# Two groups of PV products in a row every eight units, and three buffers of probabilities, in an attention and mixture-of-experts kernel

## What is computed

```python
def _L0_xattn_ref(x, c, Wq, bq, Wk, bk, Wv, bv, Wo, bo):
    q = einsum('oc,bct->bot', Wq, x) + bq        # k and v likewise, from c
    scores = einsum('bhkt,bhks->bhts', q, k) * SCALE
    p = softmax(scores, axis=-1)
    out = einsum('bhts,bhks->bhkt', p, v)
    return einsum('oc,bct->bot', Wo, out) + bo
x = x + _L0_xattn_ref(_layernorm(x), ctx, ...)   # B=8, C=256, T=512, 16 heads, 16 channels each
x = x + _L0_ffn_ref(_layernorm(x), ...)          # rmsnorm, top 2 of 8 experts, a shared expert
```

## Time and profile before

| | |
|---|---|
| median of three executions | 947.64 us (944.26 to 954.04) |
| the profiled execution's own time | 947.91 us |
| its span | 946.1 us |
| TensorE (PE) matmuls | 876.4 us, 93% of the span |
| VectorE (DVE) | 474.9 us, 50% |
| ScalarE (ACT) | 411.1 us, 43% |
| GpSimd (POOL) | 223.5 us, 24% |
| mean granted TensorE clock | 0.945 of full speed |

### The profile page before, as it was taken

How to read it: one execution, slowest core, us unless ns; L and a number is a source line. 1 busy time by engine, 2 the same in 40 slices (tenths; PEclk the granted TensorE clock), 3 DMA queues, 4 the chain that set the end, 5 groups by cost and what they waited for, 6 DMA issues and landing times. The chain is left out here.

```text
span 946.1 us, 10745 instructions
## 1 busy us (share of the span) xinstructions
PE 876.4 (93%) x3575; PEld 378.9 (40%) x3575; DVE 474.9 (50%) x915; ACT 411.1 (43%) x769; POOL 223.5 (24%) x206
## 2 busy tenths in 40 slices
PE   7798988999999999999998989987999999999992
PEld 2333423434333343333432245833544444444441
DVE  4496687687776777777784056183221111111110
ACT  1113566767667676666667741210002222222220
POOL 3113023104142031421100121000004444444431
PEclk8897899999999999999997987698999999999997
DMA  6777265456555565645611139300633555555542
GB/s 232 185 186 184 46 144 144 94 109 159 121 130 126 116 161 126 125 121 112 138 39 38 36 90 368 155 1 0 224 132 68 91 92 92 93 93 90 94 81 34
DMA packets 46872, 110.43 MB, mean 117 GB/s; under 512 B 11668, under 2 KB 12692, under 8 KB 42580
## 3 DMA queue, kind: packets, MB, share of 16 engines
q1 hardware_dynamic: 35404, 80.23, 33.6%
q0 software_dynamic: 11328, 29.37, 15.3%
q10 hardware_dynamic: 88, 0.16, 0.1%
HBM read 68.44 MB, written 41.16 MB: 116 GB/s over the span
## 5 line engine op out<-in xcount | busy, mean ns | idle before, releaser
L749 DVE TENSOR_REDUCE negmax<-smax_ps 128x1 f32<-128x512 f32 x512 | 323.4, 681 | 120.6 <-PE smax_ps L623 120.4
L549 ACT ACTIVATE probs<-st_ps 128x512 f32<-128x512 f32 x512 | 279.3, 600 | 172.5 <-PE st_ps L656 172.0
L656 PE MATMUL st_ps<-q_stack,k_stack 50*128 50x512 f32 x512 | 160.1, 501 | 13.2 <-ACT probs L549 10.9
L623 PE MATMUL smax_ps<-k_stack,q_stack 48*128 48x512 f32 x512 | 145.7, 445 | 15.1 <-DVE negmax L749 8.8
L669 PE MATMUL pv_ps<-probs,v_t 128*32 128x512 f32 x1024 | 141.2, 624 | 0.6 <-ACT probs L549 0.4
L1178 PE MATMUL big_ps<-w_gu,attn 128*128 x312 | 140.4, 593 | 0.8 <-ACT attn L1019 0.8
L656 PEld LDWEIGHTS st_ps<-q_stack,k_stack 50*128 50x128 f32 x512 | 61.5, 188 | 189.4 <-ACT probs L549 149.0
L983 POOL DMA_INDIRECT out<-x_sb,row_i x39 | 61.7, 1582 | 139.5 <-ACT x_sb L1026 132.4
L623 PEld LDWEIGHTS smax_ps<-k_stack,q_stack 48*128 48x128 f32 x512 | 68.0, 190 | 48.8 <-DVE negmax L749 33.6
L1364 DVE TENSOR_TENSOR zeros<-attn,big_ps 128x256 f32<-128x256 f32 x39 | 16.4, 421 | 134.8 <-ACT attn L1038 134.8
L1178 PEld LDWEIGHTS big_ps<-w_gu,attn 128*128 128x128 f32 x312 | 56.2, 190 | 57.0 <-issue 57.0
(11 more groups left out here) (156 smaller groups left out, 760.9 us busy)
## 6 DMA issues: line engine op xcount, KB each, us to landing
parts_dram<-parts SPq DMA_DIRECT2D x32, 512.0 KB, 6.2
k_stack<-parts_dram SPq DMA_DIRECT2D x32, 256.0 KB, 4.7
q_stack<-parts_dram SPq DMA_DIRECT2D x32, 256.0 KB, 5.3
w_gu<-in_gate_up SPq DMA_DIRECT2D x8, 1024.0 KB, 15.0
x_sb<-in_x SPq DMA_DIRECT2D x8, 512.0 KB, 7.8
c_sb<-in_ctx POOLq DMA_DIRECT2D x8, 512.0 KB, 7.8
k_stack<-parts_dram SPq DMA_DIRECT2D x32, 128.0 KB, 5.1
q_stack<-parts_dram SPq DMA_DIRECT2D x32, 128.0 KB, 5.9
```

What stands on the lines that cost most here:

```text
L549: nc.scalar.activation(probs[:, k % 2, u % GH, :], score_bank(UNITS * s + u), ACT.Exp, scale=SCALE).then_inc(exp_done, 1)
L623: nc.tensor.matmul(smax_bank(i), q_stack[buf][low:low + SROWS, pair, tt * P:(tt + 1) * P], k_stack[buf][low:low + SROWS, pair, :], start=T ...
L656: nc.tensor.matmul(score_bank(i), k_stack[buf][low:end, pair, st * P:(st + 1) * P], q_stack[buf][low:end, pair, :], start=True, stop=True, ...
L749: nc.vector.tensor_reduce(negmax[:, n % 2, c:c + 1], smax_bank(UNITS * n + u), AX_X, ALU.max, negate=True).then_inc(max_done, 1)
```

## The change

`probs` gets three buffers of one group each instead of two, and the exponentials of group k wait for `pv(k - 3)`. TensorE no longer does one group at every fourth unit, but two groups one right behind the other at every eighth: at u = 2, 10, 18 and 26, behind the two scores and the maxima of that step and ahead of whatever else hangs on it. The two copies of `pv_ps` move three units later, from after units 2 and 18 to after units 5 and 21. At the end the last two groups are done behind the loop instead of the last one.

```diff
@@ -27,6 +27,7 @@
 STBUF = 3
+PBUF = 3
@@ -108,7 +109,7 @@
-        probs = asb("probs", [P, 2, 4, T])
+        probs = asb("probs", [P, PBUF, GH, T])
@@ -544,13 +545,13 @@
                         k = STEPS * s + u // GH
-                        if u % GH == 0 and k >= 2:
-                            act.wait_ge(pv_done, k - 1)
-                        nc.scalar.activation(probs[:, k % 2, u % GH, :], score_bank(UNITS * s + u),
+                        if u % GH == 0 and k >= PBUF:
+                            act.wait_ge(pv_done, k - PBUF + 1)
+                        nc.scalar.activation(probs[:, k % PBUF, u % GH, :], score_bank(UNITS * s + u),
                                              ACT.Exp, scale=SCALE).then_inc(exp_done, 1)
-                        if u == 2 and s > 0:
+                        if u == 5 and s > 0:
                             pv_copy(2 * s - 1)
-                        if u == 18:
+                        if u == 21:
                             pv_copy(2 * s)
@@ -667,7 +668,7 @@
-                                              probs[:, k % 2, j, :], start=(st == 0), stop=(st == TT - 1),
+                                              probs[:, k % PBUF, j, :], start=(st == 0), stop=(st == TT - 1),
@@ -706,7 +707,8 @@
-                        if u % GH == 0 and STEPS * s + u // GH >= 1:
+                        if u % (2 * GH) == 2 and STEPS * s + u // GH >= 2:
+                            pv(STEPS * s + u // GH - 2)
                             pv(STEPS * s + u // GH - 1)
@@ -721,6 +723,7 @@
                             filler(smax_bank(0))
+                pv(STEPS * HALVES - 2)
                 pv(STEPS * HALVES - 1)
```

## The result

The changed kernel takes 1087.93 us, the median of four executions (1086.85 to 1091.95), against 947.71 before: a ratio of 1.148 (95% interval 1.141 to 1.155). It is 140 us slower. The forecast was 1109 us, 161 slower, from two terms: waits (67) and a falling clock (94).

The account below looks back on a forecast made before the run. PE, busy 93%, looked like the bound, but its narrow stretches were held to ACT's and DVE's pace. 947.9 us plus 67 of waits plus 94 of falling clock gave 1109 us (chance 0.71), range 1000 to 1150.

Parts of the forecast that it names:

- waits: PE held to ACT's and DVE's pace in long narrow stretches: 4.9 us a half over 12 halves, +67 us in all.
- a falling clock: PE's clock falls behind three long narrow stretches a half, slowing the next wide block by 2.6 us: +94 us (61 to 126).
- Rival 1: The clock holds in the attention loop and only the waits cost: 1015 us, 997 with small waits; chance 0.18.
- Rival 2: PE is the bound and the loop gets faster by 1.9 us a half, 27 us in all: 921 us; chance 0.03.
- switches: Changes on PE between narrow products and PV blocks: some 0.3 us saved for each block removed, 1.3 per half.
- Rival 3: The clock does not come back within a block, all wide work slow, 15 us more a half: 1195 us; chance 0.06.
- The account by rows: Sum of PE's blocks and narrow stretches in a half: 32.2 us after the change against 28.8 before, extras not included.
- The extras: ACT's and DVE's work beside units, now uncovered in long stretches (residual, statistics, copies): 1.5 us a half (0 to 2.7).
- my lower bound of 61: The low end, in us, of the range 61 to 126 given for the falling clock's cost.
- Halves 0 and 1: The first two halves of the loop, left at no added waits because DVE paces them already.
- The copies' later place: Copies of pv_ps come some 4 us later; DVE may wait for the denominators: nothing, at most 1 us a half.
- The tail: Last half and the extra PV group behind the loop 6 us, half 14 another 2: 8 us, counted in the waits.

Follow-up runs that it names:

- experiment 2: The changed kernel plus three full-width products of zeros a half, at u = 14, 24 and 30 in the long stretches: 1037.62 us, ratio 1.093 to the kernel before.
- experiments 5 and 6: 5: maxima and exponentials over half or a quarter of the columns, both kernels, 55 and 23 us apart; 6: kernel before with projections split and spread, 930.64 us.
- cut4_after: The changed kernel with VectorE's maxima and ScalarE's exponentials over a quarter of the columns: 916.47 us, against 893.63 for the kernel before with the same cut.
- cut_after: The changed kernel with VectorE's maxima and ScalarE's exponentials over half of the columns: 961.46 us, against 906.43 for the kernel before with the same cut.

## Why the prediction was right

**Direction and mechanism** held: waits and a falling clock, both through the order of wide and narrow work on PE. Rival 1 (the clock holds, 1015 us) fell with the granted clock of 0.85 and with experiment 2. Rival 2 (PE is the bound and gets its switches back, 921) fell with the result, and experiments 5 and 6 agree. Rival 3 (the clock stays low through whole blocks, 3.5 us or more in each) did not happen: no block with a projection is more than 2.84 us too long.

**The stretches.** The account by rows gave 4.39 us for eight units and 1.95 for four. The short ones around the projection at u = 6 read 1.94 in the changed kernel (360.37 to 362.31, and 364.22 to 366.16), as forecast. The block of a pair and a projection is 3.77, as forecast, and the pair in it 1.85 up to the projection (372.84 to 374.69), against the 1.86 that rested on an estimate of the last matmul's latency. The long ones of eight units between two such blocks are 4.45 to 5.25 us in even halves and 5.58 to 5.89 in odd ones. The extras, which I had put at 1.5 us a half, are 0.8 to 1.5 in even halves and 3 in odd ones (sum of the three long stretches less 3 x 4.39 and the turn), where the residual and its statistics lie in the stretch:

```profile
389.56 0.74 DVE L330 SCALAR_TENSOR_TENSOR x_sb<-proj_ps,bo_all,x_sb 128x512 f32<-128x512 f32 x1
...
391.42 0.68 DVE L794 BATCH_NORM_STATS2 stats<-x_sb 128x6 f32<-128x512 f32 x1
```

**The clock** was the term that I sized too high. I took 2.6 us for each of 36 long stretches, from blocks at half speed as in half 0: behind its narrow stretch of 4.5 us the granted clock is 0.50, also over the group at 88.11 alone (88.10 to 90.00), while the kernel before has 1.00 from 150 to 500 us, with narrow stretches like that of 1.94 in the earlier trace rows. From the turn of half 2 (175.72) to that of half 14 (643.38), 12 halves, PE's timeline has 34 blocks of a pair and a projection (from half 13 on no more keys are projected, so two of the 36 carry none). Five take 3.77 or 3.78 us. The other 29 are longer, 21 by 1.2 to 1.7 us and eight by 2.6 to 2.8. In the eight the slow level reaches into the projection, which takes 1.98 at a granted clock of 1.00; in the one below the clock is 0.50 over the pair and 0.68 over the projection (397.04 to 399.90):

```profile
393.47 3.64 PE L670 MATMUL pv_ps<-probs,v_t 128*32 128x512 f32 x16
397.04 2.89 PE L596 MATMUL proj_ps<-c_sb,w_t 128*128 128x512 f32 x4
```

Together they are 53 us too long, 1.5 for each of the 34. Four of the 14 pairs that stand alone add 6. That is 59 us against the 94 forecast, just under my lower bound of 61. No long wait of PE goes with these falls: from 176 to 500 us, at a mean granted clock of 0.86, its longest single wait is 0.71 us.

**The waits** were sized right. The 12 halves take 467.66 us against 351.68 (161.72 to 513.40), 116 more. Without the 59 that leaves 57, or 4.8 us a half, against the 59 and 4.9 forecast. It holds also what the slow clock costs inside the narrow stretches, which is not separated here. Experiment 2 agrees: its 12 halves take 421.59, and 8 us of that are blocks and fillers at the slow level, so without the slow clock they are 62 over the kernel before, fillers included. That the forecast comes so close is in part luck: at full clock a half of the changed kernel takes 34.1 us where I had 33.7, and the kernel before 29.3 where my account had 28.8, and the two errors cancel.

**What I left at nothing.** Halves 0 and 1: the turn of half 2 comes at 175.72 us instead of 161.72, 14 us late. The granted clock from 64 us to that turn is 0.77 against 0.88 before. How much of the 14 is the clock and how much waits was not separated; that VectorE paces these halves already, my reason for leaving them at nothing, did not keep them from growing. This made up for a part of the oversized clock. The copies' later place cost two waits for the denominators in the last halves, 0.6 and 1.9 us, against at most 1 us a half forecast. When ACT and DVE are cut it shows more: between 150 and 450 us DVE waited ten times for them in cut4_after, 14.2 us in all, and eleven times in cut_after up to 500, 10.7 us. That may be part of what is left of the difference there; it was not tried.

**The tail.** The last PV group ends 56.9 us behind the turn of half 14, against 43.6 before: 13 us, with 8 forecast for it and for half 14. From there to the end the changed kernel is 4 us faster (384.7 against 389.0), in the experts' block, which the change does not touch and which takes 383 to 389 us in the profiled executions here. So those 4 are no effect of the change.

**Range.** 1087.9 lies between 1000 and 1150. The sum was 21 us too high: the clock 35 too high and the waits 2, the first halves 14 and the tail 5 too low, and the 4 us of the experts' block. The number is better than its terms.

## What to carry to other kernels

Where one engine's wide work hides the others' narrow work through a few PSUM banks, what counted here is how evenly the wide blocks are spread. A block hides at most what is in the banks: under blocks of 3.77 and 5.11 us DVE had three banks to reduce and stood idle for 3.2 and 4.9 us. What follows it went at the pace of the slowest engine (5.86 us for eight units) or, with ACT and DVE cut to a quarter, of the banks' round trip (3.2). Splitting a projection cost some 0.3 us, and the kernel with split blocks is 17 us faster, so saving blocks was no reason for a longer one; and a third buffer behind the banks brought nothing (ratio 0.998), since the banks are what runs full. And before making TensorE's work sparse for some microseconds, price the clock: behind the stretch of 5.86 us it was the next wide block that paid, 3.27 us instead of 1.92 for the pair.

## What the runs showed of the hardware

That adding 41 us of useless full-width products makes a kernel 50 us faster was expected in sign only; that so few (three a half) lift the granted clock from 0.85 to 0.97 was not. PE was shown busy for 317 of 350 us (150 to 500) while the clock fell time after time; its longest single wait there was 1.8 us (at 171), and 0.71 from 176 on.

Three kernels have the same order of work and differ in the pace of ACT and DVE. From the turn of half 2 to that of half 14, in the changed kernel 29 of the 34 blocks of a pair and a projection were slow, behind stretches of 4.45 to 5.89 us; in cut_after 12 of 34, behind stretches of 3.5 to 4.55; in cut4_after one of 34, behind stretches of 3.2 to 3.7 with short waits (0.47 us at most up to 450 us). With the fillers of experiment 2 five of 34 were slow, all at u = 26, where six units (3.8 to 4.1 us) stand ahead of the filler and two behind it; in four of the five the filler itself runs slow already (1.25 to 2.0 us instead of 1.06). Whether it is the length of the narrow stretch or the waits inside that decides was not tried.
